# A four-layer graph and expert network: the third graph layer's start by row tile, an early tile count, and dense weights sooner

## The reference

```python
o1 = jnp.matmul((adj == 1).astype(jnp.float32), jnp.matmul(V, w1))
o2 = jnp.matmul((adj == 2).astype(jnp.float32), jnp.matmul(V, w2))
o3 = jnp.matmul((adj == 3).astype(jnp.float32), jnp.matmul(V, w3))
return o1 + o2 + o3 + bias
```

```python
topk_vals, topk_idx = jax.lax.top_k(gate_logits, K)     # K = 2
topk_w = jax.nn.softmax(topk_vals, axis=-1)
h = act(x @ w1[e] + b1[e]); y = h @ w2[e] + b2[e]       # for the two experts e of a row
x = x + sum(topk_w * y)
```

## Time and profile before

| What | before |
|---|---|
| median of three runs | 1123.18 us (1121.71 to 1125.84) |
| the profiled execution | 1116.28 us |
| its span on the core | 1114.5 us, 1.78 less |
| TensorE busy in the span | 965.9 us, 87% |
| VectorE busy | 712.6 us, 64% |
| ScalarE busy | 503.4 us, 45% |
| GpSimd busy | 468.2 us, 42% |
| granted clock of TensorE, mean | 0.912 |

### The profile page before, as it was taken

One profiled execution on the slowest core, in us unless ns is written; L12 is line 12 of the kernel. 1 busy time (PEld: TensorE's weight loads), 2 busy tenths in 40 slices (PEclk: granted clock), 3 DMA queues, 4 the chain that ended last, 5 costly groups with the idle time before them and its releaser, 6 DMA issues. The chain is left out here.

```text
span 1114.5 us, 22778 instructions
## 1 busy us (share of the span) xinstructions
PE 965.9 (87%) x7554; PEld 905.8 (81%) x7554; DVE 712.6 (64%) x1691; ACT 503.4 (45%) x965; POOL 468.2 (42%) x478
## 2 busy tenths in 40 slices
PE   6884999895889779958989999999899993999992
PEld 4584999685889769947989999999767883999992
DVE  4787677657777557768545456665566865566664
ACT  1341777035545347713006557777426431334431
POOL 1153686227776247710222045553134623355441
PEclk8796999898887869969999999999989996999997
DMA  6007864200000046544214001139400007755944
GB/s 246 2 29 256 291 225 161 91 1 1 11 10 11 30 164 223 180 128 137 76 57 181 11 25 39 42 116 329 162 17 1 15 15 274 246 158 169 326 159 133
DMA packets 57675, 132.30 MB, mean 119 GB/s; under 512 B 9664, under 2 KB 35712, under 8 KB 52864
## 3 DMA queue, kind: packets, MB, share of 16 engines
q1 hardware_dynamic: 47376, 106.45, 27.0%
q0 software_dynamic: 9024, 24.65, 7.3%
q10 hardware_dynamic: 1200, 0.23, 0.1%
HBM read 191.97 MB, written 17.56 MB: 188 GB/s over the span
## 5 line engine op out<-in xcount | busy, mean ns | idle before, releaser
L1898 PE MATMUL r_pH<-e_xsT,e_w 128*128 128x128 f32 x2304 | 280.1, 280 | 6.0 <-DVE e_xsT L1998 4.5
L1898 PEld LDWEIGHTS r_pH<-e_xsT,e_w 128*128 128x128 f32 x2304 | 271.7, 196 | 7.1 <-issue 6.8
L1852 POOL DMA_INDIRECT y_rows<-e_ys,e_to x94 | 156.3, 1663 | 194.6 <-DVE e_idx L2002 92.2
L1862 POOL DMA_INDIRECT e_xs<-xn_rows,e_idx x94 | 106.7, 1135 | 95.8 <-DVE e_idx L2002 50.5
L2014 DVE TENSOR_TENSOR e_w_lo<-e_w,e_w_hi 128x1024 fp32r<-128x1024 f32 (+1 forms) x94 | 137.8, 1466 | 10.8 <-ACT e_w_hi L1959 7.3
L1913 PE MATMUL r_pY<-e_w_hi,e_h_hi 128*128 128x256 f32 x464 | 138.8, 299 | 6.4 <-issue 5.8
L1913 PE MATMUL r_pY<-e_w_lo,e_h_hi 128*128 128x256 f32 x464 | 131.1, 283 | 0.0
L1913 PE MATMUL r_pY<-e_w_hi,e_h_lo 128*128 128x256 f32 x464 | 131.0, 282 | 0.0
L1959 ACT ACTIVATE e_w_hi<-e_w 128x1024 fp32r<-128x1024 f32 (+1 forms) x94 | 116.9, 1244 | 28.1 <-DMA e_w<-w_in 28.0
L503 ACT ACTIVATE g_t<-g_g,g_small 128x1024 f32<-128x1024 f32 x56 | 64.2, 1151 | 109.5 <-POOL g_small L490 109.5
L1913 PEld LDWEIGHTS r_pY<-e_w_hi,e_h_hi 128*128 128x128 f32 x464 | 88.6, 191 | 7.3 <-issue 7.3
(11 more groups left out here) (316 smaller groups left out, 1865.4 us busy)
## 6 DMA issues: line engine op xcount, KB each, us to landing
e_w<-w_in SPq DMA_DIRECT2D x56, 1024.0 KB
e_w<-w_in SPq DMA_DIRECT2D x84, 512.0 KB
e_w<-w_in SPq DMA_DIRECT2D x52, 514.0 KB
e_w<-w_in SPq DMA_DIRECT2D x24, 1028.0 KB
e_w<-y_rows SPq DMA_DIRECT2D x32, 256.0 KB, 5.3
p_adj<-adj_in SPq DMA_DIRECT2D x8, 512.0 KB, 10.8
xn_rows<-xn SPq DMA_DIRECT2D x32, 128.0 KB, 1.7
g_adjT<-adjT_in SPq DMA_DIRECT2D x8, 512.0 KB, 4.4
```

Source lines behind the costliest of these rows:

```text
L1852: pool.indirect_dma_start(out=y_rows[:, :], in_=ys[b][:, :], in_offset=None, out_offset=bass.IndirectOffsetOnAxis(ap=to[b][:, :], axis=0))\
L1862: pool.indirect_dma_start(out=xs[b][:, :], out_offset=None, in_=xn_rows[:, :], in_offset=bass.IndirectOffsetOnAxis(ap=idx[b][:, :], axis=0))\
L1898: ins = nc.tensor.matmul(pH[b % 2][:, f, :], w1[b][:, at:at + P], xsT[b % 2][:, c, :], start=(c == 0), stop=(c == DC - 1))
```

## The change

1. A new object, BeforeGraph2, takes PlainSums' place behind layer 1's feed-forward. Its buffers live in a phase n2 that is opened ahead of that step: weights, bias and the first two adjacency tiles are loaded in the feed-forward step, ahead of SP's loop. VectorE makes both tiles' masks (`vector_idle`) between its last expert tile and the bias adds. Then all engines go by row tile: add, moments, norm, transposition, projection, rounding (ScalarE, straight from PSUM), low part (VectorE), and on TensorE the products of the first result tile (product(0, c)) three tiles behind the transposition.
2. graph2 keeps result tiles 1 to 7 and the adjacency tiles from 2 on. The dense weights of layer 2 are loaded behind adjacency tile 3.
3. `more` is made early in the gate, and the loops wait for `turns_known`, not for `tiles_known` (SP's loop for both).
4. The twelve on_slot comparisons of VectorE become one of 128 x 1536; the bf16 iota is dropped.
5. In layers 0, 1 and 3 the first rise stands ahead of the second turn.
6. The transposes of the second biases go between the last rise and the falls.

```diff
+        class BeforeGraph2(Handover):
+            KINDS, AHEAD = 3, 1
...
+            def product(self, t, c):
+                for v in range(self.KINDS):
+                    for part in (self.high, self.low):
+                        ins = nc.tensor.matmul(self.pso[t % 2][:, :], self.mask[t % 2][:, v, c, :], part[:, c, v, :],
...
+            def tensor(self, pe):
+                pe.wait_ge(self.loaded, 16 * (self.KINDS + 1))
+                rouse(self.spare, 56)
+                for t in range(NT + 1):
+                    if t < NT:
+                        self.norm.turn(pe, t)
+                    if t >= 1:
+                        pe.wait_ge(self.norm.xnT_ready, t)
+                        if t >= 3:
+                            pe.wait_ge(self.split, t - 2)
+                        for v in range(self.KINDS):
+                            ps = self.psh[(t - 1) % 2][v // 2][:, v % 2, :]
+                            for c in range(DC):
+                                ins = nc.tensor.matmul(ps, xnT[:, c, (t - 1) * P:t * P], self.w[:, c, v, :],
+                                                       start=(c == 0), stop=(c == DC - 1))
+                        ins.then_inc(self.multiplied, 1)
+                    if self.AHEAD and t >= 3:
+                        if t == 3:
+                            pe.wait_ge(self.masked, 1)
+                        self.product(0, t - 3)
+                if self.AHEAD:
+                    for c in range(NT - 2, NT):
+                        pe.wait_ge(self.split, c + 1)
+                        self.product(0, c)
+
+            def scalar(self, act):
+                for t in range(NT + 1):
+                    if t < NT:
+                        self.norm.place(act, t)
+                    if t >= 1:
+                        act.wait_ge(self.multiplied, t)
+                        pair, last = self.psh[(t - 1) % 2]
+                        nc.scalar.activation(self.high[:, t - 1, 0:2, :], pair, ACT.Copy)
+                        nc.scalar.activation(self.high[:, t - 1, 2:3, :], last, ACT.Copy).then_inc(self.rounded, 1)
+
+            def vector_idle(self, dve):
+                for t in range(2):
+                    dve.wait_ge(self.adjT_loaded[t], 16)
+                    self.make_masks(t).then_inc(self.masked, 1)
+
+            def vector(self, dve):
+                link = linker(dve, self.linked)
+
+                def lower(t):
+                    dve.wait_ge(self.rounded, t + 1)
+                    pair, last = self.psh[t % 2]
+                    nc.vector.tensor_tensor(self.low[:, t, 0:2, :], pair, self.high[:, t, 0:2, :].bitcast(F32), ALU.subtract)
+                    nc.vector.tensor_tensor(self.low[:, t, 2:3, :], last, self.high[:, t, 2:3, :].bitcast(F32), ALU.subtract)\
+                        .then_inc(self.split, 1)
+
+                for t in range(NT + 2):
+                    if t < NT:
+                        self.sums.add(dve, link, t, x[:, t, :], x[:, t, :])
+                        dve.wait_ge(self.sums.ready, t + 1)
+                        self.norm.moments(dve, t)
+                    if 1 <= t <= NT:
+                        self.norm.norm(dve, t - 1)
+                    if t >= 2:
+                        lower(t - 2)
...
     graph2, VectorE:
+                        if t >= 1 and t + 1 < NT:
+                            dve.wait_ge(adjT_loaded[(t + 1) % 2], 16 * ((t + 1) // 2))
+                            if t > first:
+                                dve.wait_ge(summed, t - first)
+                            before.make_masks(t + 1).then_inc(masked, 1)
...
     gate, vector_slots:
+                nc.vector.tensor_scalar(more[:, :], turns[0:1, :], float(-HEAD), None, ALU.add).then_inc(turns_known, 1)
...
-                for q in range(POOL_SLOTS, 2 * NT):
-                    ins = nc.vector.tensor_scalar(on_slot[:, q, :], iota_b[:, :], slot_f[:, q:q + 1], None, ALU.is_equal)
-                ins.then_inc(placed, 1)
+                nc.vector.tensor_tensor(on_slot[:, POOL_SLOTS:, :], bc(iota_row[:, :].unsqueeze(1), [P, 2 * NT - POOL_SLOTS, P]),
+                                        bc(slot_f[:, POOL_SLOTS:].unsqueeze(2), [P, 2 * NT - POOL_SLOTS, P]), ALU.is_equal)\
+                    .then_inc(placed, 1)
...
     ffn, every loop:
-                    eng.wait_ge(tiles_known, 1)
+                    eng.wait_ge(turns_known, 1)
...
     ffn, TensorE:
+                        second = early(i, b, 2) and not early(i, b, 1) and not own
+                        if second:
+                            rise(*before(i, b, 1))
                         turn(i, b)
...
-                        if not early(i, b, 1):
+                        if not early(i, b, 1) and not second:
                             rise(*before(i, b, 1))
...
                     last = loop(pe, step)
+                    if biases:
+                        pe.wait_ge(biases.ready, 1)
+                        biases.turn(pe, 0)
                     rise(last, UN - 1)
+                    if biases:
+                        biases.turn(pe, 1)
                     fall(last, UN - 2)
...
     ffn, VectorE:
                     end(last, UN - 2)
                     end(last, UN - 1)
+                    after.vector_idle(dve)
                     if biases:
                         biases.add(dve, after.base)
                     after.vector(dve)
```

More of the change, by code:

```diff
@@ L337, in vector_early @@
                 pass
+            def vector_idle(self, dve):
+                pass
             def vector(self, dve):
@@ L1121, in graph2 @@
+        def graph2(before, gate_of, own_weights):
+            first = before.AHEAD
+            with Phase("g2") as ph:
                 tps = [ph.ps(f"tps{n}", [P, DC, P]) for n in range(2)]
-                psh = [ph.ps(f"psh{n}", [P, KINDS + 1, D]) for n in range(2)]
-                pso = [ph.ps(f"pso{n}", [P, D]) for n in range(2)]
-                loaded, vd, mm, split = ph.sem("loaded"), ph.sem("vd"), ph.sem("mm"), ph.sem("split")
+                psl = ph.ps("psl", [P, NT, gate_of[0]])
@@ L1153, in _ @@
                 def _(pe):
[L1154 to L1155 removed]
                     for t in range(NT):
[L1157 removed]
                         if t >= 2:
[L1159 to L1169 removed]
+                            pe.wait_ge(masked, t - 1)
                             pe.wait_ge(added, t - 1)
[L1171 removed]
+                        if t >= first:
                             for c in range(NT):
[L1173 to L1178 removed]
+                                ins = before.product(t, c)
+                            ins.then_inc(summed, 1)
                         if t >= 2:
@@ L1625, in load, with turn @@
                 sp.dma_start(self.b2[:, :], A[self.name][0:self.E, :]).then_inc(self.loaded, 16)
-            def turn(self, pe):
-                pe.wait_ge(self.ready, 1)
-                for t in range(NT):
-                    n, part = divmod(t, DC)
-                    if n >= 2 and part == 0:
-                        pe.wait_ge(self.kept, n - 1)
-                    ins = nc.tensor.transpose(self.pT[n % 2][0:self.E, part, :], self.rows[:, t, :], ident[:, :])
-                    if part == DC - 1:
-                        ins.then_inc(self.turned, 1)
-                pe.wait_ge(self.kept, NT // DC)
+            def turn(self, pe, n):
+                if n >= 2:
+                    pe.wait_ge(self.kept, n - 1)
+                for part in range(DC):
+                    ins = nc.tensor.transpose(self.pT[n % 2][0:self.E, part, :], self.rows[:, n * DC + part, :], ident[:, :])
+                ins.then_inc(self.turned, 1)
             def keep(self, act):
```

179 lines of the change are left out of this document (79 added, 100 removed).

## The result

The changed kernel takes 1144.95 us (median of four runs, 1140.7 to 1151.3), the kernel before 1124.51 (four runs, 1121.71 to 1126.07): a ratio of 1.0177 with a 95% interval of 1.0129 to 1.0224, so 20 us slower, within 15 to 25. The forecast was +14, 1137, with a range of 1118 to 1148.

A forecast was written before the change was run, and what follows sets the result against it. TensorE, busy for most of the span, was taken as the bound, with its idle places as the target. Seam +17.9 and entry gains -3.8 gave +14.1 us on the 1123.18 median: 1137, range 1118 to 1148.

The forecast's parts named there:

- The chain: Loop by row tile: norm, turn, projection, rounding, lower, add, moments, norm form a closed chain; links sum to 6.9 us.
- The period of 8.2: One round of the loop by row tile, with turn and projection taking 4.1 in place of 2.84; range 6.9 to 9.7.
- A + 59.8 + 6 P: Time of layer 2's last adjacency sum, P being the loop's period; it was A + 92.6 before.
- A: End of layer 1's expert bias adds, where the seam starts; forecast 1.5 us later because six mask passes precede the adds.
- The clock: Loop by row tile: TensorE's waits of at least 3.2 us lower its clock to about 0.69 for turn and projection.
- The rival that let it fall in every round for all of its work: Loop by row tile: period 9.7, seam +26.9, whole +23.1, 1146 us; chance 0.10.
- the one that let it hold: Loop by row tile: clock stays up despite waits of 3.2, period 6.9, whole +6.3, 1129.5 us; chance 0.20.
- The graph step: Layer 2, behind the loop: 43.6 us again, plus TensorE's second row tile 1.2 late for the third mask's adjacency tile.
- The gains at the entries: Expert loops: 0.3 in layer 0, 0.5 in layer 1, 1.0 in layer 3, 2 x 1.0 from bias transposes: -3.8 us.
- a rival with 0.06: Expert loop entries: VectorE's one comparison holds up GpSimd, 1 us at each entry, +3 on the forecast, 1140; chance 0.06.
- The swap of the first rise: Layer 3's entry: first rise comes sooner but the second waits for its own copy; -1.0 us, ends 0 and -2.
- The three rises' gain of 10.6: Entries of layers 0, 1, 3: sooner gathers reach first rises at full clock; rival giving 1112 to 1124, chance 0.20.

The follow-up runs named there:

- the four rounds with the clock held up: 36 or 28 useless matmuls added on TensorE at the end of each loop round, against the changed kernel: 1141.43 us, ratio 1.0174.
- the five profiles with this loop: Changed kernel unedited, twice (1144.95, 1144.87 us), and with prefetch behind the loop's weights (1141.51), comparisons as before (1143.54), or first rise behind second turn (1141.79).
- the second profile: The changed kernel profiled once more with no edit: 1144.87 us.

## Why the prediction was right, and where not

**The chain.** Right, link by link. In the round at the full clock the turn takes 0.27 to the projection, that 2.80 to the rounding, that 0.90 to the low part, that 0.94 to the add, and the add, moments and norm 2.03 to the next turn: 6.94, where the prediction had summed 6.9 from rows of other places; it is 6.94 again in the four rounds with the clock held up.

**The seam's size.** The period of 8.2 was 7.98, and 8.19 over the rounds that have all links. That it came out so well is in part luck: the same five rounds average between 7.6 and 8.5 in the five profiles with this loop, and single ones go from 6.9 to 9.7. By the formula A + 59.8 + 6 P the seam would be 107.7 with 7.98; it is 110.1, and 112.3 in the second profile. What is missing in the first is in the ends. The first turn came 6.2 behind A and not 5.3, because the 56 useless matmuls ahead of it took 6.08 (the earlier trace rows has 4.84) and the turn stands behind them. And the last turn is 9.3 ahead of the loop's end, not 8.3: six products of the first tile stand between the last two projections, 0.9 that the sum doesn't have. It also overlooked, on the other side, that the last period has no add and no moments in it. The prediction's +17.9 has the 1.5 of A in it, so from A alone it stands for +16.4, and the "17 to 18 later behind A" of its last paragraph counts A's move a second time.

**The clock.** Right in kind. Waits of 3.2 to 3.9 were followed by the lower clock in some rounds and not in others (0.68, 0.81, 1.00, 0.79). The rival that let it fall in every round for all of its work, and with it the Trainium skill's "Every single K-tile." (TensorE: Matmul & The Clock Gate, section "HAM oscillation — how this bites in real kernels"), was met by one round in four; the one that let it hold, by another.

**The graph step.** Right: the turn behind the first tile there waits 1.21 for VectorE's norm, which waits behind the masks of the late adjacency tile; the sum had 1.2.

**A.** Right in its cause, 1.5 forecast, 2.2 and 1.3 measured.

**The gains at the entries.** -3.8 forecast, about +4 measured in the profiles. What is shown to be wrong is the prefetch; of the rest the profiles and the medians say different things.
- Layer 1's prefetch was set at -0.5 with ends of -2 and +2, and that entry measured +3.5 and +3.9. I had taken the bytes as a shared load, and a shared load it was, but set it too small: the gather's turn came 8.3 behind its start in place of 3.5, with the DMA engines busy for 0.98 of the time.
- The bias transposes inside the last tiles were to give 1.0 each in layers 0 and 2. The adds do start 1.05 sooner behind the last fall, but three of the four pairs of transposes now lie ahead of that fall on TensorE, and the fall itself comes later (from the first to the last fall in layer 0 81.0 and 81.8 before, 81.9 and 83.5 after; in layer 1 67.3 and 67.5, and 67.6 and 67.7 after). So most of it looks like a move and not a saving, but the profiles of one kernel differ by as much.
- The comparison was set at 0, with +1.5 as its end, and cost 1.2, 0.8 and 1.2 at the table. The rule of the Trainium skill (SBUF — State Buffer, section "SBUF: two separate sides"), that two inputs from SBUF on VectorE shut GpSimd out, agrees with these runs: the comparison of GpSimd that starts with VectorE's 1.75 takes 2.1 to 2.2, and 0.6 with the old form. I had it as a rival with 0.06; it was the case at every one of the three entries, but the first falls of layers 0 and 3 don't show its price.
- By the medians the change without its seam and prefetch is 3.3 faster than the kernel before. That is what the forecast has for these gains without the prefetch (3.8 less 0.5), though no stretch shows them; whether they are there stays open.

**The swap of the first rise.** The wait of the second rise for its copy was named; it cost 0.7 in layer 3 where -1.0 was taken.

**The rivals' prices.** The three rises' gain of 10.6 is 9.9 by the numbers given for it (4.8 for the clock and 5.1 for the gathers). No forecast rests on it.

**The total.** +14.1 forecast, +20.4 measured. The time of 1145 lies within the range, but in the band that the prediction gave to the fully fallen clock (1142 to 1150, 0.10), and not for that rival's reason, rounds of 9.7 throughout. By the profiles the seam with A gave +20.3 where +17.9 was forecast, layer 1's entry +3.7 where -0.5 was, layer 3's +0.7 where -1.0 was, and the gains of layer 0's entry and of the biases, 2.3 together, don't show. That is 24.7; the medians have 4 less, and the traces don't tell where.

## What to carry to other kernels

When stages over all tiles are made into one loop by tile, write down each engine's order in a round and follow who waits for whom: if the path returns to its start within a round, the period is the sum of its links, whatever the engines' loads. Taking the last link one round later cost nothing here and took a round from 8.0 to 3.5 us. And a prefetch is not free because its queue has time for it: here it filled the DMA engines while a gather that the next stage waited for was on another queue. Issued behind the loop's loads it cost nothing that the rows show.

## What was not expected of the hardware

Two executions of the same kernel before differ by 8.2 us of span, with single stretches up to 5.9 us apart; a difference of a few microseconds between two single profiles says little without a second profile of each. And VectorE's one comparison of 1536 elements, itself quicker than twelve of 128 (1.75 against 2.1), made the pair of engines slower: GpSimd's four took 4.34 us as a group in layer 1 and 4.88 in layers 0 and 3, where it had been 2.87 and 2.99.
